# Two-stream local attention on one core: the keys of a layer rotated, normed and scaled ahead of its queries, with a new order of merging the streams

## What is computed

```python
def _layer(x, wqkv, qs, ksc, wo, lg, lb, w1, b1, w2, b2):
    h = shift_token(x)                    # half of the features come from the token before
    q, k, v = split(h @ wqkv)             # 8 heads of 64
    q = l2norm(q) * qs
    k = l2norm(k) * ksc
    q, k = rotary_xpos(q, k)
    o = local_attention(q, k, v)          # windows of 64 tokens, each sees itself and the one before
    x = x + o @ wo
    h = layernorm(shift_token(x)) * lg + lb
    a, g = split(h @ w1 + b1)
    return x + (a * gelu(g)) @ w2 + b2
```

## Time and profile before

| what | value |
|---|---|
| median of 3 runs | 1343.25 us (1342.24 to 1343.5) |
| the profiled execution | 1344.58 us, its span 1342.2 us |
| PE busy | 1093.8 us (81%) |
| PEld busy | 569.9 us (42%) |
| DVE busy | 978.8 us (73%) |
| ACT busy | 912.8 us (68%) |
| POOL busy | 466.6 us (35%) |
| mean granted TensorE clock | 0.935 of full speed |
| the second part | from some 469 us to the end |

### The profile page before, as it was taken

The page is one execution under the profiler, slowest core; times in us unless marked ns, Lnnn a source line. Parts: engine busy times, 40 slices in busy tenths (PEclk is TensorE's granted clock), DMA queues, the critical chain, the costliest instruction groups (busy, mean ns, idle before and its releaser), DMA issues. The chain is left out here.

```text
span 1342.2 us, 24422 instructions
## 1 busy us (share of the span) xinstructions
PE 1093.8 (81%) x8120; PEld 569.9 (42%) x8120; DVE 978.8 (73%) x1937; ACT 912.8 (68%) x2746; POOL 466.6 (35%) x524
## 2 busy tenths in 40 slices
PE   4588888888888668988878789787888887888886
PEld 3233233233232235555545555454544454454553
DVE  5989888988988777668567586575775766856843
ACT  1588897898888736766646667566576574766662
POOL 2000000000000057357254464362653634545630
PEclk9699998999999979999888999888999998899988
DMA  5442241340331001110101101101001010111010
GB/s 182 161 126 64 64 126 32 94 118 25 109 103 23 0 0 30 29 29 1 37 0 37 28 2 29 36 1 36 9 21 29 1 37 0 37 29 29 1 29 16
DMA packets 24546, 59.04 MB, mean 44 GB/s; under 512 B 2736, under 2 KB 2928, under 8 KB 23280
## 3 DMA queue, kind: packets, MB, share of 16 engines
q1 hardware_dynamic: 24432, 57.62, 15.2%
HBM read 23.98 MB, written 18.87 MB: 32 GB/s over the span
## 5 line engine op out<-in xcount | busy, mean ns | idle before, releaser
L544 ACT ACTIVATE E<-slot,neg_max 128x512 f32<-128x512 f32 x512 | 344.2, 731 | 76.8 <-DVE neg_max L828 68.8
L828 DVE TENSOR_REDUCE neg_max<-slot 128x2 f32<-128x1024 f32 x256 | 306.0, 1212 | 39.6 <-PE slot L1072 39.5
L1072 PE MATMUL slot<-v_rows,k_rows 128*128 128x512 f32 x512 | 214.1, 489 | 61.1 <-ACT E L544 50.5
L477 POOL TENSOR_TENSOR rot_work<-rot_work,rz 128x512 f32<-128x512 f32 x128 | 133.2, 1042 | 325.0 <-DVE rz L889 324.9
L603 ACT ACTIVATE rot_work<-bank,neg 128x128 f32<-128x128 f32 x512 | 181.2, 376 | 64.6 <-DVE neg L884 41.6
L1072 PEld LDWEIGHTS slot<-v_rows,k_rows 128*128 128x128 f32 x512 | 92.1, 197 | 245.4 <-ACT E L544 213.2
L1120 PE MATMUL bank<-wqkv_sb,hs 128*128 128x512 f32 x384 | 188.2, 617 | 8.3 <-DVE rot_work L863 4.8
L463 POOL TENSOR_TENSOR work<-work,rot_work 128x512 f32<-128x512 f32 x128 | 162.9, 1273 | 78.3 <-DVE rot_work L863 74.4
L455 POOL TENSOR_TENSOR qz<-qT,rz 128x32 f32<-128x32 f32 x128 | 30.7, 240 | 416.9 <-DVE rz L832 416.9
L1082 PE MATMUL o_bank<-E,qz 128*32 128x512 f32 x1024 | 143.6, 635 | 1.7 <-POOL qz L455 1.7
L472 POOL TENSOR_TENSOR work<-work,rn 128x512 f32<-128x512 f32 x128 | 131.2, 1061 | 23.4 <-DVE rn L786 23.4
(11 more groups left out here) (120 smaller groups left out, 1652.4 us busy)
## 6 DMA issues: line engine op xcount, KB each, us to landing
v_rows<-v_scr SPq DMA_DIRECT2D x8, 1024.0 KB, 6.4
k_rows<-k_scr SPq DMA_DIRECT2D x32, 256.0 KB, 7.4
work<-v_al SPq DMA_DIRECT2D x16, 512.0 KB, 4.4
work<-v_al SPq DMA_DIRECT2D x16, 384.0 KB, 6.6
k_scr<-hi SPq DMA_DIRECT2D x16, 256.0 KB, 3.0
k_scr<-lo SPq DMA_DIRECT2D x16, 256.0 KB, 3.2
v_scr<-hi SPq DMA_DIRECT2D x16, 256.0 KB, 3.1
v_scr<-lo SPq DMA_DIRECT2D x16, 256.0 KB, 3.5
```

Of the source, the lines that this page charges most:

```text
L477: pool.tensor_tensor(pr[s][:, u % PR_SLOTS], pr[s][:, u % PR_SLOTS], rz2[s][:, u, :].unsqueeze(2).broadcast_to([P, 4, 2 * W]), ALU.mult).t ...
L544: act.activation(E[:, g % E_RING, 2 * half + m, :], slot[:, m], ACT.Exp, bias=neg_max[:, n, m:m + 1], accum_out=z[:, n, m:m + 1]).then_inc ...
L828: dve.tensor_reduce(neg_max[:, n, :], slot[:], AX.X, ALU.max, negate=True).then_inc(max_ready, 1)
L1072: last = pe.matmul(bank, k_rows[:, hh, q, P * j:P * (j + 1)], v_rows[:, par, q, :], start=True, stop=True)
```

## The change

1. Each stream projects k0, v0, k1, v1, k2, v2, k3, v3 and then q0 to q3. Squarings, rotations and additions go by the new list `ROTATIONS`: k0 to k3, then q0 to q3.
2. The norm is done twice in a layer pass, for k alone and for q alone: clamp, Ln and Exp, and the Newton step work on `[:, :, w, :]`, 32 elements a partition each, in place of 64 once. On VectorE the clamp of k stands after the rotation of k3 and the Newton step of k after the rotation of q0. On ScalarE Ln and Exp of k stand after the squaring of q1.
3. GpSimd scales k0 after it has added q0, k1 after q1, and so on; then it scales q0 to q3.
4. TensorE transposes k0 to k3 and then q0 to q3; their banks and ScalarE's copies are in that order. The V shift waits for the last q transposes' bank.
5. The one semaphore for scaled blocks becomes two, `k_ready` and `q_ready`.
6. All merge strings are new. VectorE's is 32 steps longer, ScalarE's 16; TensorE's and GpSimd's keep their number of steps, and SyncE's string is the same.

```diff
+ROTATIONS = [(i, w) for w in (1, 0) for i in range(J)]
-B_CHAIN = LN_CHAIN + (2 + LN_CHAIN) * L
+B_CHAIN = LN_CHAIN + (2 * 2 + LN_CHAIN) * L
...
         for i in range(J):
-            out += [("q", l, i), ("k", l, i), ("v", l, i)]
-        for i in range(J):
-            out += [("qT", l, i), ("kT", l, i)]
+            out += [("k", l, i), ("v", l, i)]
+        out += [("q", l, i) for i in range(J)]
+        out += [(name, l, i) for name in ("kT", "qT") for i in range(J)]
...
             def b_shift_v(s, k, l):
-                b_done(sp, s, k, ("kT", l, J - 1))
+                b_done(sp, s, k, ("qT", l, J - 1))
...
-            def b_scale(s, k, l, n):
-                i, w = divmod(n, 2)
-                if n == 0:
-                    pool.wait_ge(rn_ready[s], k * L + l + 1)
-                    passed(pool, rot_sum[s], (k * L + l + 1) * 2 * J)
+            def b_scale(s, k, l, i, w):
+                if i == 0:
+                    pool.wait_ge(rn_ready[s], (k * L + l) * 2 + 2 - w)
+                passed(pool, rot_sum[s], (k * L + l) * 2 * J + J * (1 - w) + i + 1)
...
                         for n in range(2 * J):
                             b_rotary(s, now[s], l, n)
                             yield
-                        for n in range(2 * J):
-                            b_scale(s, now[s], l, n)
+                            if n >= J:
+                                b_scale(s, now[s], l, n - J, 1)
+                                yield
+                        for i in range(J):
+                            b_scale(s, now[s], l, i, 0)
                             yield
...
-            def b_norm(s, k, l):
-                act.wait_ge(ss_all[s], k * L + l + 1)
-                act.activation(nlog[s][:], ss[s][:], ACT.Ln).then_inc(ss_log[s], 1)
+            def b_norm(s, k, l, w):
+                act.wait_ge(ss_all[s], (k * L + l) * 2 + 2 - w)
+                act.activation(nlog[s][:, :, w, :], ss[s][:, :, w, :], ACT.Ln).then_inc(ss_log[s], 1)
...
                             b_square(s, now[s], l, n)
                             yield
-                            if n % 2:
-                                b_values(s, now[s], l, n // 2)
+                            if n < J:
+                                b_values(s, now[s], l, n)
                                 yield
-                        b_norm(s, now[s], l)
+                            if n == J + 1:
+                                b_norm(s, now[s], l, 1)
+                                yield
+                        b_norm(s, now[s], l, 0)
...
-            def b_norm(s, k, l):
-                passed(dve, ss_ready[s], (k * L + l + 1) * 2 * J)
-                dve.tensor_scalar(ss[s][:], ss[s][:], NORM_MIN2, SHIFT2, ALU.max, ALU.mult).then_inc(ss_all[s], 1)
+            def b_norm(s, k, l, w):
+                passed(dve, ss_ready[s], (k * L + l) * 2 * J + J * (2 - w))
+                v = ss[s][:, :, w, :]
+                dve.tensor_scalar(v, v, NORM_MIN2, SHIFT2, ALU.max, ALU.mult).then_inc(ss_all[s], 1)
...
                             b_rotate(s, now[s], l, n)
                             yield
-                        b_norm(s, now[s], l)
+                            if n == J - 1:
+                                b_norm(s, now[s], l, 1)
+                                yield
+                            if n == J:
+                                b_rnorm(s, now[s], l, 1)
+                                yield
+                        b_norm(s, now[s], l, 0)
                         yield
-                        b_rnorm(s, now[s], l)
+                        b_rnorm(s, now[s], l, 0)
```

More of the change, by code:

```diff
@@ L88 @@
     "PE": (
[L89 to L93, removed]
@@ L94 @@
[L94 to L96 removed]
+        "xxxxxxxxxxxxxxxxxxxxxyxxyyxyxyxxxyyxyxxxyyxyyxyxxyxyxyyyxyyyyxyxxxyxxxyxyyyxxyxyyyxxxxxxxyxyxyyxyxyx"
+        "xyxxxxxyxyyyyxxyyyxxxyxyyxxyyxyxyyyyxxxyxyxyyyxyyyyyxyxxxxyxxyxyyxyyyyxyyxxxxxxyxxxyxyyxyxxxyxxxyxxx"
@@ new lines @@
+        "xyxyyyxyyyxyxxyxxxyxxyyyyyyxyyyyyxxxyxyyxyyxyyyyyxyxxxyyxxxxyyyxyxxxxyyyxxyxxxyxyyxyxyxxyxxxxxyxxyyy"
+        "yxxyyyxxxyyyyyyxxxxyxyyyyxxxyyxyxyyyxyyyyxyxxxxxxyxyyxyyyyxyyxxxxxxyxxxxxyyyxxyxyxxxyxxxxyxyyyxxyyyy"
+        "xxxyxxxxyxyyyyyyyyyyyxxxyyxyxyyxyyyyyxyxxxyxxxyxyyxyyxxxxxyxxyyxxyxyyyxyxxyxxxyxxxxyxyyyxxyyyyxxxyyy"
+        "yxxxxyyyyyyyxxxxyxyxyyyxyyyyyxyxxxxxxyxyyxyyyyxyyxxyxxxxxxxxxxyyyxyxyxxxyxxxxyxyyyyxxyyyxyxxxxyxxyyy"
+        "yyyxyyyyyyxxxyxyxyyyxyyyyxyxxxyyxxxxyyyxxxxxyyyyxxxyxxyyyxxyxxyxxyxxxxxyxyyyxyyxyyxxxyxyyyyyxxxyyxyy"
@@ L97 @@
+        "xxxyxyxyyyxyyyyyxyyxxxyxyyyyxxxyyyyxyyyyyyyyyyyyyyyy"
     ),
     "DVE": (
[L99 to L102, removed]
@@ new lines @@
+        "yxyxxxyxxxyxyyyyyyyxyyxyyxxxxyyyyyyyxxxyxxyyyyyxxxyyyyyxxyxxyxxyxxyyxyyxxxxxxxyyyxyyxxxxxyyyxxxxxyyx"
+        "yyyyyxxyyxxxxyyyyyyyxxxyxyxxyyyxyyyxyyyxyxxxxxxxxxyyxxyyyyxxxxxxxyyyxyxxxxxyyxyxxxxyxyyyyyyyyyxxyyyx"
+        "xxxyyyyyyyxxxyxxyyyyyxxxyxxyyyyxyxxxxyyxxyyyyxxxxxxxyyyxyyxxxxxyyxxxxxyxyyyyyxyxyyyxxxxyyyyyyyxxxyxy"
+        "yxxyyyxyyxyyyxyxxxxxxxxxyyxxyyyyxxxxxxxyyyxyxxyyxxxyxxyxxxyxyyyyyyyxyxyyyxxxxyyyyyyyxxxyxxyyyyyxxxyy"
+        "yyyxxyxxxxyyxxxyyyyxxxxxxxyyyxyyxxxxxyyyxxxxxyyxyyxyxyyyxxyxxyyyyyyyyyyxyyxxyxyyyyyxyyyyyyyyyyyy"
@@ L106 @@
     ),
     "ACT": (
[L108 to L112, removed]
@@ L113 @@
-        "yyxyyyyxxyyxyxxxxyyxxxxxxyxxyxxyxxxyxyxxyxxyyxyxxyyxyxxyyxyyxyxxyxyxxyyxxyyyyxyyyyxyxyyyyxyxyyxxyxxx"
-        "xyyyxxyxxyyxyxyxxxxyxxxyxyxxyxyyxxyyxyyxxyxxyyxxyxyyxxyxyxyyyyxyyyyyyyxyyyyyxyyyyyyyyyyy"
+        "xxxxxxxxxxxxxxxxxxxxxxyxxxyyxxxxxxyyyyxxxxyyyxyxyxyyxxyxyyyyxyyyyyxyxyyxyyyyxyyxyxxyyxyxxyxxxxxyyxyx"
+        "xxxyxxxxyxxyxxyxxxxyxxyxyyxyxyxyxyyxyyxyxyyyxyyyyyxyyyxyxyyyyyyyxyyxxyxyxyxxxxyxxxyxxyxxxxxyxxxxxyxy"
+        "xxyxxxxxxyxxyyxyxyxyyyyxyyyyyxyxyyyyxyyyyxyyxyyxyyyyxyyxyxxyxxyxxyyxyxxyxxyxxxyxxxxyxxxyxxyxxxxyxxyx"
@@ L115 @@
+        "yyyyyxxxyxyyxyyyxxyyyyxyyyyyxyxyyxyyyyyyxyyxxyxyxyxxxxyxxxxxyxyxxxxyxxxxxyxyxxyxxxxxxxxyxxyyxyxyyyyy"
+        "yyyyyxyxyyyyxyyyyxyyxyyxyyyyxyyxxyxyxxxxyyxxyyxxyxyxxxxyxxxxxyxyxxyxxxxyxxyxyyyxxxyxyyyyyyxxyxyyyxyy"
+        "yyyyxyxyyxyyyyyyxyyxxyxyxyxxyxxxxxxxxyyxxxxxyxxxxyxyxxyxxxxxxyxxyyxxyyxyyyyxyyyyyyxxyyyyyxyyyyxyxyyx"
+        "yyyyxyyxyxxxxyyxyxyxxyxxyyxxxxxyxxxxyxxyxxyxxxxyxxyxxyyyyyxxyxyxyyxyxyyyxyyyyyxyyyxyyyyyyxyyyyyyyyyy"
+        "yyyy"
     ),
     "POOL": (
-        "xxxxxxxxxxxxxxxxyyxxxyyxyxyyxxyxyyyyyyyyyyyyxxyxxxyxyxyxxxxxxxxxxxxxxyyyyxyxyxyyyyyyyyyyyyyyyyyxxxxx"
@@ L121 @@
+        "xxxxxxxxxxxxxxxxyyyyyyyyyyyyyyyyyyyyyxxxxyyxyxxxxxxxxxxxxxxxxyyxxyxyyyyyyyyyyyyyyyyyyyyxyxxxxxxxxxxx"
+        "xxxxxxxxxxxyxyyyyyyyyyyyyyyyyyyyyxxxyyxyxxxxxxxxxxxxxxxxxyyyxxyxyyyyyyyyyyyyyyyyyyyy"
     ),
@@ L268, in build @@
         ss_all, ss_log, ss_rsqrt, rn_ready = sems("ss_all"), sems("ss_log"), sems("ss_rsqrt"), sems("rn_ready")
-        qk_ready = sems("qk_ready")
+        k_ready, q_ready = sems("k_ready"), sems("q_ready")
         v_pad = sems("v_pad")
@@ L460, in b_rotary @@
             def b_rotary(s, k, l, n):
-                i, w = divmod(n, 2)
+                i, w = ROTATIONS[n]
                 b_done(pool, s, k, ("qk"[w], l, i))
@@ L579, in b_values @@
                 act.activation(v_al[s][:, i, :], bank[:], ACT.Copy).then_inc(free, 1)
-            def b_norm(s, k, l):
-                act.wait_ge(ss_all[s], k * L + l + 1)
-                act.activation(nlog[s][:], ss[s][:], ACT.Ln).then_inc(ss_log[s], 1)
-                act.wait_ge(ss_log[s], k * L + l + 1)
-                act.activation(rn[s][:], nlog[s][:], ACT.Exp, scale=-0.5).then_inc(ss_rsqrt[s], 1)
+            def b_norm(s, k, l, w):
+                act.wait_ge(ss_all[s], (k * L + l) * 2 + 2 - w)
+                act.activation(nlog[s][:, :, w, :], ss[s][:, :, w, :], ACT.Ln).then_inc(ss_log[s], 1)
+                act.wait_ge(ss_log[s], (k * L + l) * 2 + 2 - w)
+                act.activation(rn[s][:, :, w, :], nlog[s][:, :, w, :], ACT.Exp, scale=-0.5).then_inc(ss_rsqrt[s], 1)
             def b_heads(s, k, l, i):
@@ L637, in b_stream @@
                             yield
-                            if n % 2:
-                                b_values(s, now[s], l, n // 2)
+                            if n < J:
+                                b_values(s, now[s], l, n)
                                 yield
-                        b_norm(s, now[s], l)
+                            if n == J + 1:
+                                b_norm(s, now[s], l, 1)
+                                yield
+                        b_norm(s, now[s], l, 0)
                         yield
                         for i in range(J):
+                            b_keys(s, now[s], l, i)
+                            yield
+                        for i in range(J):
                             b_heads(s, now[s], l, i)
-                            yield
-                            b_keys(s, now[s], l, i)
                             yield
@@ L1116, in b_project @@
```

(9 more changed lines are left out.)

24 lines of the change are left out of this document (11 added, 13 removed).

## The result

The changed kernel takes 1324.9 us at the median (1323.64 to 1326.36), the kernel before 1343.4 in the same runs: ratio 0.986, 95% interval 0.9841 to 0.9878. So 18.5 us are gone; 24 were forecast.

A forecast was written before the change was run, and what follows sets the result against it. TensorE was taken as nearest to the bound, its idle time after 469 us to be won. Terms -9 - 10 - 12 + 6 - 3 = -28, taken as -24: 1344.6 - 24 - 1.3 = 1319.5 us, range 1299 to 1344.

The forecast's parts named there:

- three wait terms: TensorE's waits before the second layer norm transposes, before the head transposes and in the softmax pipeline: -9, -10 and -12 us.
- Scaling chain: From R, the end of a stream's last rotation in a layer, to the last scaled Q: 2.8 us sooner, at R + 7.6.
- Price of the new steps: K's norm and Newton steps on VectorE, waiting for GpSimd's current instruction: 0.8 + 1.4, 2.2 us per layer and stream.
- Rotation stretch: VectorE's rotations beside the other stream's softmax: net +0.4 us a half-turn, +6 us over 15.
- 1.8 us less: Other-stream softmax instructions among VectorE's rotations: the new merge order has three fewer, of 0.60 us each.
- L1127: TensorE's 13.6 us wait before the head transposes, for GpSimd's scaling: three quarters go, -10 us.
- no wait for L472 of more than a few us: Sign that the forecast is right: TensorE waits there no more than a few us in total.
- L1187: TensorE's 35.5 us wait before the second layer norm transposes: about 0.9 of each 2.5 us goes, -9 us.
- Softmax waits: TensorE's 61.3 us of waits inside the softmax pipeline: a fifth goes as exponentials start earlier, -12 us; least certain term.
- Ends: First batch and the last stream running out, together: +2.2 - 2.8 - 2.8 = -3.4, taken as -3 us.
- half-turns: Spans between the streams' last rotations, a first stretch (31.0 us) then the rotations (18.6): -1.6 in 49.6 us.
- VectorE as the bound: Rival: VectorE bounds the rotations, each new small step waits for a different GpSimd instruction; +27, some 1370 us; chance 0.14.

The follow-up runs named there:

- no_newton_k: The changed kernel without the Newton step of K, so K is scaled by the unrefined reciprocal root: 1308.7 us, ratio 0.9725 to the kernel before.
- no_clamp: The changed kernel without VectorE's clamps for K and Q, factor moved into ScalarE's Ln, lower bound left out: 1313.5 us, ratio 0.9772 to the kernel before.
- fill_old: The kernel before with eight unread identity transposes on TensorE ahead of the wait for the second layer norm transposes: 1334.2 us, ratio 0.9928.

## Why the prediction was right, and where its terms were not

The direction, the size and the range held. That the total came out near is in part luck: the three wait terms were to bring 31 us and brought 6, and a source that the forecast doesn't have, the clock, brought 13.0. By its own steps:

- **Scaling chain.** Forecast: last Q ready at R + 7.6, 2.8 us sooner. Measured over the 16 passes: R + 6.6 to 7.5, against 10.3 to 11.0 before. Right, and a little better.
- **Price of the new steps.** Forecast 0.8 + 1.4; measured 0.72 for the clamp of K and 1.33 for its Newton step. Right, by the wait for GpSimd's instruction. no_newton_k shows that the Newton step is paid nearly in full; of the clamps, K's and Q's together, no_clamp shows half.
- **Rotation stretch, +0.4 us.** Mis-sized. From the first rotation to R the 15 passes after the first take 20.4 us at the mean, 18.1 before: +2.3. The new steps add 2.1. The "1.8 us less" of the merge was read from one place. Over the 15 passes, 1.5 maxima fewer but 0.8 head copies more stand among the rotations, some 0.4 us saved. And VectorE stands still 1.0 us more in the stretch, 0.8 of it before a rotation, for ScalarE's squarings; the forecast has no term for that wait.
- **L1127, -10 us.** Wrong in sign: +34. The term that failed is "Of the 13.6 us before L1127 three quarters go". K's transposes and Q's now come where TensorE has little other work behind them, and they go at GpSimd's pace of 1.03 us a block. The sign of being right, no wait for L472 of more than a few us, did not come.
- **L1187, -9 us.** Right in mechanism, too small: -27.7 and a wait of 7.8 us where 26 were forecast. In 12 of 15 gaps the first score block stands there, as forecast, and K's and Q's last transposes are spread over the gap by GpSimd's pace: part of this gain is the loss at L1127.
- **Softmax waits, -12 us.** The size is right, the way is not. The four waits of the forecast went from 61.3 to 33.1 + 3.2 + 7.4 + 5.1 = 48.8 us, -12.5. But the wait of the score blocks for the exponentials, which were to start earlier, doubled from 17.5 to 33.1, and the one for the copies of probabilities fell from 18.4 to 3.2. Beside them the score blocks' wait for the head copies, which is not in the sum, grew from 3.3 to 12.6.
- **Ends, -3 us.** Right: R of the first pass comes 1.3 us later (488.2 for 486.9), and from the last R to the end it is 66.7 us for 71.7: -3.7.
- **What was left out.** The clock. The waits in these terms sum to 4.5 us more than before, all of TensorE's waits to 6.4 less, and the time fell by 19.6 because the waits that are left are short: 69 waits of 0.7 us for GpSimd in place of 14 of 2.5 us before L1187. I had the 0.93 of the earlier trace rows before me and counted a wait at its length. 13.0 of the 19.6 us came as faster matmuls, 10.2 of them in the projections right behind the wait that shrank; fill_old shows that filling this wait alone speeds them up. What remains argued is how much of the lower clock time elsewhere hangs on which wait.

So half-turns fell by 15.9 us in 15, 1.1 each, where 1.6 were forecast. Of the rivals, VectorE as the bound was the nearest. Its price is real, 18 us for the Newton step alone, and two of its signs came: the rotation stretch is over 20 us at the mean and grew by more than 1.5. In the half-turn shown the first stretch is 30.8 us for 31.0, but over all of them it shrank by 3.4 us at the mean, and so the half-turns still fell. No value product waits for the V shift among TensorE's waits, and the Q scalings started at R + 2.3 to 3.2, inside the bound of 4.5.

## What to carry to other kernels

With orders written out by hand for two streams, test a restructuring against a new merge of the old steps: here the merge alone gives nearly three times what the change gave, and the change's steps add nothing to it that two searches show. Count a wait on TensorE by its length and by what the granted clock does behind it; many short waits can be cheaper than few long ones of the same sum. Idle filler is a quick test, and costs time where there is no wait. A small VectorE instruction from SBUF to SBUF that meets a running GpSimd instruction costs that one's remainder, here 0.76 us at the median for 0.15 us of work. Folding such a clamp into ScalarE gave 10 us with the old order and nothing that shows once the order was searched anew.

## What the hardware showed that I had not expected

Eight useless transposes a layer pass made the kernel 10 us faster: the projections behind them ran at the full clock in 9 of 16 passes, in 6 without. And a clamp on 64 numbers a partition cost 0.8 us at its place, 10 us over the kernel before. All 16, even the shortest at 0.29 us, ended 49 to 55 ns behind a GpSimd addition; none ran free.
